# The value matmuls of three attention layers as column tiles, with the softmax sums inverted on GpSimd and a later projection

## The reference, cut to what matters

```python
x = x + jnp.tanh(g_xattn[1]) * _L1_xattn_ref(_layernorm(x, axis=-1), ctx_1024, ctx_1024, ...)
...
q = _split_heads(Q @ Wq + bq)
k = _split_heads(K @ Wk + bk)
v = _split_heads(V @ Wv + bv)
scores = jnp.einsum('bhqd,bhkd->bhqk', q, k) * scale
P = jax.nn.softmax(scores, axis=-1)
O = jnp.einsum('bhqk,bhkd->bhqd', P, v)
...
return O @ Wo + bo
```

## Time and profile before

| | |
|---|---|
| median of 3 runs | 1611.73 us (1611.02 to 1615.39) |
| the profiled execution, its time | 1615.22 us |
| its span | 1613.4 us |
| PE busy | 1379.8 us, 86% |
| DVE busy | 1221.0 us, 76% |
| ACT busy | 770.3 us, 48% |
| POOL busy | 371.8 us, 23% |
| value matmuls (L1131), PE busy | 137.8 us in 1024 records, four layers |

### The profile page before, as it was taken

How to read it: one execution, slowest core, us unless ns; L and a number is a source line. 1 busy time by engine, 2 the same in 40 slices (tenths; PEclk the granted TensorE clock), 3 DMA queues, 4 the chain that set the end, 5 groups by cost and what they waited for, 6 DMA issues and landing times.

```text
span 1613.4 us, 25827 instructions
## 1 busy us (share of the span) xinstructions
PE 1379.8 (86%) x9858; PEld 1262.5 (78%) x9858; DVE 1221.0 (76%) x2365; ACT 770.3 (48%) x1314; POOL 371.8 (23%) x294
## 2 busy tenths in 40 slices
PE   4897997698898479999489679968989999999995
PEld 4786896576796379999479568856977889999994
DVE  5696778789597769877369888976986857888873
ACT  4446342111455256777355522425554225676672
POOL 2242001011000046774200341000010012454432
PEclk9898998789899579999699989978998999999997
DMA  4332100010001268887400000000002026777783
GB/s 141 91 105 76 60 19 1 1 37 18 11 1 76 89 208 226 234 233 213 140 1 1 8 0 1 1 10 1 2 7 100 1 92 238 226 205 229 212 246 114
DMA packets 45438, 148.23 MB, mean 92 GB/s; under 512 B 11651, under 2 KB 22582, under 8 KB 35574
## 3 DMA queue, kind: packets, MB, share of 16 engines
q1 hardware_dynamic: 30038, 124.93, 22.6%
q0 software_dynamic: 15296, 21.90, 7.5%
HBM read 126.03 MB, written 22.87 MB: 92 GB/s over the span
## 4 chain that ended last, share of the span: by engine, by line
PE 60%; DVE 23%; ACT 6%; issue 4%; DMA 3%; POOL 1%; POOLq 1%; SPq 1%; ACTq 0%; DVEq 0%
PE PS L307 41%; PE PS L1131 6%; PE PS L1093 3%; PE PS L1115 3%; DVE X L2178 2%; PE PS L1366 1%; DVE RA L297 1%; PE PS L1124 1%; PE PS L1772 1%; ACT Y L225 1%; DVE RA L1750 1%; POOLq L2930 1%; ACT RA L482 1%; DMA FA<-in_Wo 1%; DVE FA L2666 1%
## 5 line engine op out<-in xcount | busy, mean ns | idle before, releaser
L307 PE MATMUL PS<-RA 128*128 128x256 f32 (+3 forms) x6204 | 939.5, 311 | 79.6 <-DVE RA L397 16.9
L307 PEld LDWEIGHTS PS<-RA 128*128 128x128 f32 x6204 | 855.8, 197 | 136.4 <-issue 47.7
L1677 POOL DMA_INDIRECT sum_rows<-Y,KT x78 | 145.9, 1871 | 195.0 <-ACT Y L1718 162.3
L271 POOL TENSOR_TENSOR rstd<-vareps,neghalf 128x4 f32<-128x4 f32 x36 | 36.8, 1023 | 516.0 <-DVE vareps L208 221.9
L1666 POOL DMA_INDIRECT Y<-normed_rows,KT x78 | 95.2, 1221 | 217.8 <-DVE KT L1459 157.1
L1131 PE MATMUL PS<-VBF,FA 128*128 128x136 f32 x1024 | 137.8, 289 | 3.9 <-ACT FA L898 3.8
L1131 PEld LDWEIGHTS PS<-VBF,FA 128*128 128x128 f32 x1024 | 126.8, 195 | 9.4 <-ACT FA L898 6.0
L1750 DVE TENSOR_TENSOR RA<-FA,RA 128x2048 fp32r<-128x2048 f32 x46 | 105.3, 2289 | 10.9 <-ACT RA L1710 10.7
L898 ACT ACTIVATE FA<-PS 128x1024 f32<-128x1024 f32 x64 | 65.6, 1025 | 99.9 <-PE PS L1093 99.9
L1696 ACT ACTIVATE FA<-PS,unit_bias 128x256 f32<-128x256 f32 (+1 forms) x184 | 71.4, 443 | 79.9 <-PE PS L307 68.6
L1819 DVE TENSOR_TENSOR RA<-FA,RA 128x1024 fp32r<-128x1024 f32 (+1 forms) x46 | 80.9, 1759 | 24.7 <-ACT RA L1743 24.7
(11 more groups left out here) (314 smaller groups left out, 1882.7 us busy)
## 6 DMA issues: line engine op xcount, KB each, us to landing
FA<-in_eup SPq DMA_DIRECT2D x46, 1024.0 KB, 7.5
FA<-in_edown SPq DMA_DIRECT2D x23, 1024.0 KB, 6.5
FA<-in_edown SPq DMA_DIRECT2D x23, 512.0 KB, 4.0
FA<-in_fside SPq DMA_DIRECT2D x16, 512.0 KB, 3.6
sum_rows<-X SPq DMA_DIRECT2D x2, 2048.0 KB, 7.3
normed_rows<-Y SPq DMA_DIRECT2D x2, 2048.0 KB, 10.1
FA<-fp_rows SPq DMA_DIRECT2D x1, 2112.0 KB, 11.9
X<-in_x SPq DMA_DIRECT2D x4, 512.0 KB, 9.3
```

Source lines behind the costliest of these rows:

```text
L307: ins = pe.matmul(dst, stat(a, k), mov(b, k), start=(first and n == 0), stop=(last and n == len(todo) - 1))
L1677: pool.indirect_dma_start(out=sum_rows, in_=rows_out[p][:, t, :], in_offset=None, compute_op=ALU.add, out_offset=bass.IndirectOffsetOnAxis ...
```

## The change

In layers 1 to 3:

- The operands of the value matmuls change places. `VB` (now 34 columns per pair of heads: 32 of values, 2 of ones) is stationary with 32 columns, the transposed probabilities move, and the result goes to 32 partitions, one column tile of four. A second set of eight matmuls has ones (`head_ones`) as the stationary operand, so the sums come out repeated over the 16 partitions of their head. The output stands with heads on partitions at once: the transposes are gone.
- ScalarE copies outputs and sums (128 x 512) to SBUF. GpSimd raises the 256 sums per partition to the power -1, multiplies, and later subtracts the high part for the low part. ScalarE makes the high part from the normalised output.
- The projection of a tile comes three slots after its values instead of one (`TO_Y`), and a matmul with a selecting operand `sel_r` adds the output bias in PSUM. VectorE's share in a slot is the update of X, the maximum, the subtraction and the statistics; the latter follow two slots later than before.
- In layer 2 the first group's fp4 steps on GpSimd go one to a slot.

Layer 0 keeps its order, with value matmuls of 34 columns, each for itself.

```diff
-VC = P + HC
+VW = 2 * DK
+VC = VW + 2
...
+            def gpsimd_step(self, pool, g, n):
+                u, m, x = self.u, self.m[g], self.x(g)
+                if n == 0:
+                    pool.wait_ge(self.scaled, g + 1)
+                    pool.tensor_tensor(self.blocks(u), self.blocks(x), self.of_block(self.rs[g]), ALU.mult).then_inc(self.divided, 1)
...
-            FIRST_SLOT, LAST_SLOT = -LEAD - 1, NT + 1
+            FIRST_SLOT, LAST_SLOT = -LEAD - 1, NT + (1 if first else 3)
+            TO_Y = 1 if first else 3
...
+                    def outputs_lo(t):
+                        pool.wait_ge(ot_hi, T + t + 1)
+                        pool.tensor_tensor(ots[t % 2][:, 1], ors[t % 2][:, 0:D].rearrange("p (k t) -> p k t", k=KC),
+                                           ots[t % 2][:, 0].bitcast(F32), ALU.subtract).then_inc(ot_split, 1)
+
+                    for t in range(NT):
+                        o, inv = ors[t % 2][:, 0:D], ors[t % 2][:, D:2 * D]
+                        pool.wait_ge(o_copied, T + t + 1)
+                        pool.tensor_tensor(inv, inv, negone[:, :].to_broadcast([P, D]), ALU.pow).then_inc(inverted, 1)
+                        pool.wait_ge(inverted, T - NT + t + 1)
+                        pool.tensor_tensor(o, o, inv, ALU.mult).then_inc(o_norm, 1)
+                        if t:
+                            outputs_lo(t - 1)
+                        if t >= 7 and t % GT == 3:
+                            following.pool_rstd(pool, t // GT - 1)
+                        if l == 2 and t >= 13:
+                            rows_of_fp4.gpsimd_step(pool, 0, t - 13)
+                    outputs_lo(NT - 1)
+                    if l == 2:
+                        rows_of_fp4.gpsimd_step(pool, 0, 3)
+                    following.pool_rstd(pool, NG - 1)
...
+                    if not first and slot.has(-1):
+                        t, p = slot.tile(-1)
+                        slot.wait(act, o_ready, -1, 1)
+                        slot.wait(act, ot_split, -1, -1)
+                        act.activation(ors[p], PS[:, 6, :], ACT.Copy).then_inc(o_copied, 1)
...
+                    if not first and slot.has(-2):
+                        t, p = slot.tile(-2)
+                        slot.wait(act, o_norm, -2, 1)
+                        slot.wait(act, y_ready, -2, -1)
+                        act.activation(ots[p][:, 0], ors[p][:, 0:D].rearrange("p (k t) -> p k t", k=KC), ACT.Copy).then_inc(ot_hi, 1)
...
-                            steps(dve.tensor_tensor(tmp, y, bo_row, ALU.add))
                             x = X[:, bass.ds(t, 1), :]
-                            dve.scalar_tensor_tensor(x, tmp.unsqueeze(1), gates[:, l:l + 1], x, ALU.mult, ALU.add).then_inc(fin_done, 1)
+                            dve.scalar_tensor_tensor(x, y.unsqueeze(1), gates[:, l:l + 1], x, ALU.mult, ALU.add).then_inc(fin_done, 1)
...
+                        if not first:
+                            pe.matmul(PS[:, 7, D:2 * D], sel_r, bo_r, start=True, stop=False)
...
+                        if slot.has(-TO_Y):
+                            project(-TO_Y)
+                        if slot.has(0):
+                            t, p = slot.tile(0)
+                            slot.wait(pe, pt_sb, 0, 1)
+                            slot.wait(pe, o_copied, 0, 0)
+                            for k in range(KC):
+                                for at, weights in ((k * P, VB[:, t // HT, 4 * k:4 * k + 4, 0:VW]),
+                                                    (D + k * P, head_ones.unsqueeze(1).to_broadcast([P, 4, VW]))):
+                                    for c in range(4):
+                                        ins = pe.matmul(PS[c * VW:(c + 1) * VW, 6, at:at + P], weights[:, c, :],
+                                                        pt[:, 4 * (c // 2) + 2 * k + c % 2, :], start=True, stop=True)
+                            ins.then_inc(o_ready, 1)
```

More of the change, by code:

```diff
@@ L371, in gpsimd @@
                                 allow_small_or_imprecise_dtypes=True))
-                for c in range(H // 2):
-                    for half in range(2):
-                        at = P + 2 * (c % 4) + half
-                        steps(pool.memset(VB[half * S2:(half + 1) * S2, :, c, at:at + 1], 1.0))
+                for half in range(2):
+                    rows = slice(half * S2, (half + 1) * S2)
+                    steps(pool.memset(VB[rows, :, :, VW + half:VW + half + 1], 1.0))
+                    steps(pool.memset(head_ones[rows, half * DK:(half + 1) * DK], 1.0))
                 self.all_consts = steps.n
@@ L491, in scalar_keys @@
                         vd = VD[rows, self.l, b, :].rearrange("p (c t d) -> p t c d", t=2, d=DK)[:, half]
[L492 to L495 removed]
+                        ins = act.activation(VB[rows, b, :, half * DK:(half + 1) * DK], vd, ACT.Copy)
                 ins.then_inc(self.keys_ready, 1)
@@ L711, in attention @@
             wo = rview(9216, 2, KC, D)
-            ot = rview(10240, 2, KC, P)
+            ots = [rview(at, 2, KC, P) for at in ((10240, 10240) if first else (10240, 8576))]
+            ors = [fview(8192 + 2 * D * p, 2 * D) for p in range(2)]
             qs = rview(15360 if l == 2 else 11776, 2, KC, TOK)
@@ L906, in work @@
                         act.activation(pr, pr, ACT.Exp).then_inc(p_ready, 1)
-                    n = slot.first + slot.p - 7
+                    n = slot.first + slot.p - (7 if first else 9)
                     if not first and 0 <= n < EARLY_TILES:
@@ L1118, in work @@
                         ins.then_inc(s_ready, 1)
-                    if slot.has(-1):
-                        t, p = slot.tile(-1)
-                        slot.wait(pe, o_norm, -1, 1)
-                        slot.wait(pe, fin_done, -1, 0)
-                        for k in range(KC):
-                            ins = pe.transpose(PS[:, 7, k * P:(k + 1) * P], osb[:, p, k * P:(k + 1) * P], ident[:, :])
-                        ins.then_inc(ot_ready, 1)
-                    if slot.has(0):
-                        t, p = slot.tile(0)
-                        slot.wait(pe, pt_sb, 0, 1)
-                        for k in range(KC):
-                            for c in range(4):
-                                ins = pe.matmul(PS[:, 6, k * VC:(k + 1) * VC], pt[:, 4 * (c // 2) + 2 * k + c % 2, :],
-                                                VB[:, t // HT, 4 * k + c, :], start=(c == 0), stop=(c == 3))
-                        ins.then_inc(o_ready, 1)
@@ L1134, in work, with project @@
-                    if slot.has(-1):
-                        slot.wait(pe, ot_split, -1, 1)
-                        if slot.first + slot.p == 1:
-                            pe.wait_ge(wo_ready, l + 1)
-                        split_matmuls(pe, PS[:, 7, D:2 * D], range(KC), lambda a, k: ot[:, a, k, :],
-                                      lambda m, k: wo[:, m, k, :]).then_inc(y_ready, 1)
+                    def project(d):
+                        t, p = slot.tile(d)
+                        slot.wait(pe, ot_split, d, 1)
+                        slot.wait(pe, fin_done, d, 0)
+                        if t == 0:
+                            pe.wait_ge(wo_ready, 2 * l + 1)
+                        if not first:
+                            pe.matmul(PS[:, 7, D:2 * D], sel_r, bo_r, start=True, stop=False)
+                        split_matmuls(pe, PS[:, 7, D:2 * D], range(KC), lambda a, k: ots[p][:, a, k, :],
+                                      lambda m, k: wo[:, m, k, :], first=first).then_inc(y_ready, 1)
```

122 lines of the change are left out of this document (78 added, 44 removed).

## The result

The changed kernel takes 3480.82 us (median of 4 runs, 3477.44 to 3481.84), beside 1611.38 for the kernel before in the same session (4 runs, 1608.85 to 1615.39): 2.163 times as long, interval 2.159 to 2.166. The prediction said 1615, in a range of 1572 to 1990: wrong. What happened is its last rival, the power priced per element (of a partition, as experiment 1 shows), with 0.15 of chance and about 3800 us.

A forecast was written before the change was run, and what follows sets the result against it. It took TensorE's full queue, 4.82 us a slot, as the bound. Terms +2 (slots), -4.7 (layer 2), +3.3 (tails), +2.4 (fp4), +1 (bias low part), -1 (layer 0) gave +3 on 1611.7: 1615 us, range 1572 to 1990.

The forecast's parts named there:

- last rival: GpSimd's power priced fully per element: slot 51 us, 48 x 46 = +2200, about 3800 us; chance 0.15.
- I take 1.4: the row is nearest as it stands, a price of a call: GpSimd's power at 256 elements: fixed price 1.02 from the 4-element row plus 0.4 at the plain rate, 1.4 us.
- What waits: With a power above 3.1 us, TensorE waits for GpSimd's split before the projection, values and next transposes queued behind.
- one matmul per 0.11: Value matmuls on TensorE: column tiles overlap only from one matmul to the next, sixteen taking 1.91 us a slot.
- the other bound: Value matmuls on TensorE with no column tiles overlapping: 32 x 0.109 = 3.49 us.
- rival of four tiles at once: Value matmuls in 0.92 us, slot 4.0, ScalarE and waits keeping it near 4.05: 1576 us; chance 0.18.
- a shape of its own: Value matmuls on TensorE: entering and leaving their own tiled shape adds 0.30 us a slot.
- Its reader comes a slot or more later: GpSimd's 1.02 us power for the following norm, every fourth slot, stands behind the tile's work; its reader comes later.
- The tail: Layer's end, last value matmuls to last projection: 4.9 us where 3.43 stood; +1.1 per layer, 3.3 in all.
- -4.7: Layer 2, slots 11 to 15: VectorE's slow update of X is relieved; 5.7 us too many, 1 kept for fp4.
- +2.4: Layer 2's end: a 2.4 us fp4 step on GpSimd stands between the last multiply and the last subtract.
- -1 taken: Layer 0's value matmuls shrink from 136 to 34 columns: 1.8 us saved at most, -1 taken.

The follow-up runs named there:

- experiment 1: Changed kernel with the power on 128 x 128 in layer 1, 64 x 256 in layer 2, exponent -1/2 in layer 3: 3152.03 us.
- one_tile: plain with all value matmuls of layers 1 to 3 sent to one column tile, rows 0 to 31: 1700.84 us.
- plain: Changed kernel with a multiplication by -1 in the place of GpSimd's power: 1591.09 us, ratio 0.988 to the kernel before.
- experiment 5: Changed kernel with VectorE's reciprocal, inverting only part: 1614.01 us; inverting all, with the norm's small power ahead of a tile's work: 1615.02; the same move on plain: 1575.57.
- plain_early: plain with GpSimd's small power for the following norm moved ahead of a tile's work: 1575.57 us, ratio 0.979 to the kernel before.
- before_again: The kernel before, word for word, profiled once more: 1608.1 us.
- plain_again: plain, word for word, run and profiled once more: 1584.52 us.
- experiment 7: Kernel before with 34-column value matmuls in all layers: 1623.16 us, repeated 1633.62; also unchanged repeats, before_again and plain_again, to compare stretches at the lower clock.

## Why the prediction was wrong

- **The step that failed**, in its own words: "I take 1.4: the row is nearest as it stands, a price of a call". At 256 columns the power takes 41.12 us: a call's price of 0.39 and 0.159 for every column. The other reading was the right one: all of the 1.02 us beyond the plain call goes with the four columns, 0.19 us each by that sum against 0.159 measured, slot 51 against 43.4. The row spoke for it: the plain operations show 0.26 over for the call, 0.76 us were left for four columns, and that it "repeats to a few ns" says nothing on size. The time would follow: 48 x (43.37 - 4.82) = +1850, beside the +1869 measured.
- **What waits**: right as to the place. TensorE waits for the split before the projection, at a lower clock.
- **The column tiles**: "one matmul per 0.11", 1.91 in all, was wrong. From the values to the next group it is 1.02, near the bound of 0.92, since records start four at a time; one_tile showed the other bound right (3.61 to the next group, 3.49 said). This is the rival of four tiles at once (slot 4.0, measured 3.97); its ScalarE limit of 4.05 did not bite.
- **The other TensorE terms** hold. With 0.92 for the values the four groups' terms make 3.71; the measured 3.97 leaves 0.26 for "a shape of its own", where 0.30 was taken.
- **"Its reader comes a slot or more later"**, of the small power: wrong. It is read in the same slot, and the reader waits 2.2 to 5.0 us at the head of VectorE's queue; moving the power took 3.2 to 5.1 us a layer off plain (experiment 5).
- **The tail**: 4.9 us were predicted from the last values to the last projection; plain has 8.5 (498.74 to 507.24) and plain_early 5.9 (496.96 to 502.87). The sum had 1.4 for the power where plain's multiplication takes 0.61, so not 3.6 but 4.4 are missing. 2.6 of them go with that small power, which there also holds up the update of X. The sum also lacks the update of tile 14, which must read the bank before the last projection writes it: in both runs TensorE waits 0.67 for it. The rest was not taken apart.
- **Layer 2**: the update of X takes 0.39 to 0.48 again, no longer 1.74, and most of "-4.7" came: in plain the last four slots take 17.9 us, 2.0 over four times 3.97, where before had 5.7 too many. But from the last values to the last projection layer 2 takes 3.0 us more than layer 1 in plain, against "+2.4". There GpSimd's small power and fp4's third step (2.34 us) stand ahead of the last low part, and VectorE waits 5.01 for that power. So layer 2's attention is still 6.4 us longer than layer 1's (84.9 and 78.5), as it was 7.0 before (95.2 and 88.2) and 4.1 in before_again.
- **Layer 0**: "-1 taken"; the slots save 0.07 each, and still it is 5.7 us longer in plain than before, up to layer 1's first scores. Of these, 4.2 are what plain has over plain_again, the same program at a mean granted clock of 0.89 instead of 0.87 over that stretch, so the clock is the likely cause. For the other 1.5, at before's clock of 0.89, no run shows a cause (experiment 7).

Shown by experiment are the power's price, its part in the loss, what the tiles and their order are worth, VectorE as the bound at 4.71, and the price of the small power's place. Of layer 2 and the tail the rows are read, and no run took their parts away one by one; the clock's stretches stay open.

## What to carry to other kernels

Before an operation is used at a new size, its price must be known at two sizes: the row of a 4-column instance left it anywhere between 1.4 and 49 us, and the product with 48 slots then decided everything. An engine with 3% of its time used, as GpSimd in the earlier trace rows, is free only for work whose rate is known. A small operation at the end of one engine's round can hold a full engine for 2.5 us; look at who reads it next, and put it ahead of the round's long work if its input is there (26 us here, for two moved lines).

## What the chip showed that I had not expected

- GpSimd's power: 0.39 us + 0.159 us per column, the same for 64 and 128 partitions and for exponents -1 and -1/2.
- VectorE's reciprocal: 0.14 us + 6.25 ns per column, the same for 64 and 128 partitions, where a subtraction of 1024 columns takes 1.22, 1.2 ns a column.
- Four column tiles of 32 columns give 32 f32 records in 1.08 us with the tile as innermost loop, 2.46 tile after tile, 3.68 in one tile.
- After a pause of 2.2 to 4.0 us on TensorE the lower clock level lasted from 3 to 19 us for like work, twice it didn't come, and it was not always the same in two executions of one kernel.
